# New places in the round for the small pieces of a batch, and shifted values copied by DMA

## The chip, the cores and the metric

The kernel runs on one core of a Trainium2 chip. The metric is the time of one execution on the device, in microseconds; three runs of the kernel before gave 1841.18, 1840.72 and 1837.23 us, median 1840.72. One further execution was profiled.

## What is computed

One transformer layer in float32 on 8 batches of 1024 tokens with 128 features: a relative-position attention with 8 heads of 16 features, then a mixture of 8 experts of which each token uses two.

```python
xh = xn.reshape(b, s, H, Dh)
q = xh @ Wq + bq
k = xh @ Wk + bk
v = xh @ Wv + bv
p = pe @ Wp
content = jnp.einsum('bqhd,bkhd->bhqk', q + u_bias, k)
pos_score = jnp.einsum('bqhd,khd->bhqk', q + v_bias, p)
pos_score = _rel_shift(pos_score)
attn = jax.nn.softmax((content + pos_score) / jnp.sqrt(jnp.float32(e)), axis=-1)
ctx = jnp.einsum('bhqk,bkhd->bqhd', attn, v).reshape(b, s, e)
x = x + ctx @ Wo + bo
```

After it, for each token, a small router (a projection to 64 features, a normalization, a GELU, 8 logits, the best two of them) and, for each expert, `(x1 * gelu(x2)) @ W2`, weighted and added to x. The relative shift moves each row of the position scores by one more column than the row above; along the diagonal it needs, for each key, the value of the token behind it ("shifted values", the values of tokens 1 to 1024 in the places 0 to 1023).

## The kernel before, in words

The program has a prologue, an attention loop of 8 rounds (one for each batch), a tail, and an expert phase that the change doesn't touch. The loop is one body, written out and repeated with a branch. A round is written as 8 heads `h` of 9 units `u`; a place `(h, u)` in the tables is a unit of the round. In every unit all engines have their own list of work in the same order:

- TensorE (block `pe`): `second_pass` computes two halves of 512 scores into `pB` for the softmax of head h (L612 to L626), and `first_pass` two pieces of 512 scores of head h + 2 into one of three banks `pA` (L586 to L604), in turns. In the units 1, 4, 6 and 8 (`PAIRS_AT`, L217) 16 context matmuls (L637) follow, which weigh the values with the probabilities of two key blocks. The units 0, 2, 3, 5 and 7 have no context matmuls. In unit 8 the first pass is 8 small matmuls (L604).
- ScalarE (`act`): two exponentials of 512 columns (L906, L908) out of `pB` into one of four probability buffers, or into `upper_diag` in unit 0.
- VectorE (`v`): reads each `pA` bank with a mask and keeps maxima (L974, L980 in unit 8); TensorE waits before `first_pass` for the bank it writes (`s1_read`).
- GpSimd (`po`): masks the diagonal blocks (L487 to L499), and issues DMAs: `store` (L427, the operands of the next batch to DRAM) and `scatter` (L452, rows of tokens to their experts).
- SyncE (`sp`): loads the operands of a head three heads ahead (`stack`), the row of maxima (`maximum_row`), the odd and even rows exchanged (`swap`, L249), x in and out.

Between these each round has its small pieces, at places set by tables (L178 to L216). The larger ones on TensorE: "turn" (transposes of the context), "project" 0 and 1 in the table `W_ORDER` and `M_ORDER` (the output projection, L667), "shifted" (values of the tokens moved by one, L573), eight pieces of `project()` for the next batch (two transposes L547, then q, p and k in halves of 512 columns, L550), all in head 2 in the units 0 to 7; "rows", "hidden", "fold", "logits", "ranks" of the router (L675 to L702), `upper_form` (L557), "super" (L561) and "values" (L567). The small ones are "row" (L578, the maxima of a head) and "context" (L583). Pieces write one of two banks, `pM` or `pE`. Each has a reader on ScalarE or VectorE, and TensorE waits in its queue until the bank was read (`m_done`, `w_done`, `e_done`) before the next piece for that bank. ScalarE reads pieces (`evacuate`, L811 to L818; `copied`, L840 and L848) ahead of the exponentials of the unit after the piece.

On VectorE, `normalized` (L1007 to L1015) works on the context of the batch before in head 0; its last step, at (0, 7), multiplies `vsh` by `den` (L1015). `router_apply` (L1043) scales the tokens for the router, two tiles each at (2, 5) to (2, 8), `low` (L958) makes the low parts of the operands, `stats` and `normalize` belong to the layer norm of the next batches. On GpSimd `residual` (L431, at (0, 6)) adds the bias to the residual, `positions` (L410 to L417) rotates, `rstd` (L385 to L397) takes inverse roots in head 7.

The engines meet only at semaphores. TensorE and the others execute strictly in the order written, so a place in a table is a place in every queue.

## Time and profile before

| | us |
|---|---|
| median of three runs | 1840.72 |
| profiled execution | 1844.59 |
| its span, first to last instruction | 1843.0 |
| TensorE busy in the span | 1640.6 |
| VectorE busy | 1439.7 |
| ScalarE busy | 1087.3 |
| GpSimd busy | 1145.3 |
| mean granted TensorE clock | 0.929 of 2.4 GHz |

The attention loop begins near 103 us (the second exponential of its first unit) and its last exponential ends at 1357.8 us; the rest of the span is the prologue, the tail of the attention and the expert phase. Times in the trace are counted from the start of the span. A unit is delimited here by the start of its second exponential (L908) and of the next unit's. The matmuls of TensorE are recorded with an overlap, so its busy share near 100% says that it had work, not that its array was full; idle time of an engine and what ended it stand behind an instruction in the timeline.

### The profile page before, as it was taken

How to read it: one execution, taken by the hardware profiler on the slowest of the kernel's cores; microseconds unless marked ns; L12 is line 12 of the kernel's file. 1: busy time of each engine (PE TensorE's matmuls, PEld its weight loads, DVE VectorE, ACT ScalarE, POOL GpSimd, SP SyncE). 2: the span in 40 equal slices, each digit the busy share in tenths (PEclk: the TensorE clock that was granted, in tenths of full speed). 3: DMA queues.
4: the chain of work that ended last, by engine and by line, in shares of the span. 5: the costliest groups of instructions: out<-in, count | busy, mean ns of one | idle time of the engine just before them, and what ended most of it. 6: DMA issues, size and time to landing. Idle time of an engine off the chain costs nothing. (4 is left out here: it accounts for less than half of the span.)

```text
span 1843.0 us, 50545 instructions
## 1 busy us (share of the span) xinstructions
PE 1640.6 (89%) x12522; PEld 1246.7 (68%) x12523; DVE 1439.7 (78%) x5415; ACT 1087.3 (59%) x2162; POOL 1145.3 (62%) x2136
## 2 busy tenths in 40 slices
PE   2689999999999999999999999999962699999997
PEld 1466666666676666667666666766641599999997
DVE  3578978988888887898889789888964477777775
ACT  2046666655665665666566566656630466666665
POOL 4156666767657676765766667576673266665665
PEclk8579999998998999999899999999975799999999
DMA  4425523633643363264256236426444233333333
GB/s 162 153 79 144 141 77 111 157 104 91 155 99 103 109 158 97 83 154 115 83 136 150 75 89 160 107 79 171 114 131 131 42 49 52 52 48 51 52 48 45
DMA packets 138828, 191.53 MB, mean 104 GB/s; under 512 B 27424, under 2 KB 102064, under 8 KB 138576
## 3 DMA queue, kind: packets, MB, share of 16 engines
q1 hardware_dynamic: 91088, 126.67, 25.1%
q0 software_dynamic: 47488, 61.99, 17.2%
q8 instruction: 99, 1.62, 0.4%
q14 instruction: 153, 1.25, 0.2%
HBM read 108.24 MB, written 75.06 MB: 99 GB/s over the span
## 5 line engine op out<-in xcount | busy, mean ns | idle before, releaser
L974 DVE CUSTOM_DVE_ANT_0 junk<-pA,lmask 128x512 bf16<-128x512 f32 x1056 | 689.7, 682 | 184.9 <-PE pA L598 93.3
L1443 POOL DMA_INDIRECT out<-yb,dst x144 | 234.2, 1627 | 162.4 <-ACT yb L1517 86.8
L598 PE MATMUL pA<-K,QL 96*128 96x512 f32 (+3 forms) x792 | 290.2, 368 | 16.2 <-DMA K<-split_operands 14.9
L906 ACT ACTIVATE prob<-pB 128x512 f32<-128x512 f32 x384 | 229.1, 597 | 111.2 <-PE pB L619 86.3
L621 PE MATMUL pB<-QL,K 97*128 97x512 f32 (+3 forms) x768 | 286.6, 373 | 0.0
L619 PE MATMUL pB<-QU,K 97*128 97x512 f32 (+3 forms) x640 | 270.5, 423 | 5.4 <-ACT b_all L906 2.9
L600 PE MATMUL pA<-K,QU 96*128 96x512 f32 (+3 forms) x660 | 245.5, 373 | 26.5 <-DVE acc L974 18.8
L637 PE MATMUL pC<-prob,vext 128*32 128x256 f32 x3088 | 231.9, 405 | 1.5 <-POOL prob L499 1.5
L908 ACT ACTIVATE prob<-pB 128x512 f32<-128x512 f32 x384 | 229.1, 596 | 3.5 <-PE pB L621 2.8
L499 POOL TENSOR_TENSOR prob<-prob,upper_diag 128x128 f32<-128x128 f32 x384 | 185.8, 484 | 32.3
L452 POOL DMA_INDIRECT routed_rows<-rows_r,idx x156 | 158.0, 1013 | 51.0 <-issue 26.7
L619 PEld LDWEIGHTS pB<-QU,K 97*128 97x128 f32 x640 | 123.4, 193 | 94.8 <-issue 35.6
L598 PEld LDWEIGHTS pA<-K,QL 96*128 96x128 f32 x792 | 157.1, 198 | 38.6 <-DMA K<-split_operands 15.2
L600 PEld LDWEIGHTS pA<-K,QU 96*128 96x128 f32 x660 | 136.0, 206 | 50.9 <-DVE acc L974 32.7
L1555 DVE SCALAR_TENSOR_TENSOR g<-pLin,b_all,gl 128x256 f32<-128x256 f32 x292 | 126.0, 478 | 53.5 <-PE pLin L1466 51.2
L621 PEld LDWEIGHTS pB<-QL,K 97*128 97x128 f32 x768 | 153.2, 199 | 15.4 <-issue 3.9
L492 POOL MEMSET prob<- 1x1 f32 x384 | 34.7, 90 | 189.8 <-ACT prob L908 188.0
L637 PEld LDWEIGHTS pC<-prob,vext 128*32 128x32 f32 x3088 | 90.2, 114 | 87.5 <-issue 36.7
L1510 ACT ACTIVATE gl<-pGate,b_all 128x256 f32<-128x256 f32 x292 | 122.2, 470 | 45.3 <-PE pGate L1466 45.1
L1472 PE MATMUL pY<-w_all,g 128*128 x1152 | 140.4, 275 | 0.0
L487 POOL TENSOR_SCALAR_AFFINE_SELECT upper_diag<-upper_diag 128x1024 f32<-128x1024 f32 x64 | 70.0, 1094 | 111.2 <-ACT upper_diag L908 110.2
L1472 PEld LDWEIGHTS pY<-w_all,g 128*128 128x128 f32 x1152 | 134.2, 192 | 0.0
(304 smaller groups left out, 3741.2 us busy)
## 6 DMA issues: line engine op xcount, KB each, us to landing
QL<-split_operands SPq DMA_DIRECT2D x67, 256.0 KB, 3.5
QU<-split_operands SPq DMA_DIRECT2D x67, 256.0 KB, 3.9
K<-split_operands SPq DMA_DIRECT2D x67, 256.0 KB, 4.1
xg<-routed_rows SPq DMA_DIRECT2D x76, 132.0 KB, 2.2
QL<-split_operands SPq DMA_DIRECT2D x67, 128.0 KB, 3.5
QU<-split_operands SPq DMA_DIRECT2D x67, 128.0 KB, 3.8
K<-split_operands SPq DMA_DIRECT2D x67, 128.0 KB, 3.9
split_operands<-c_h POOLq DMA_DIRECT2D x16, 512.0 KB, 6.2
```

Of the source, the lines that this page charges most:

```text
L452: po.indirect_dma_start(dram["xs"], bass.IndirectOffsetOnAxis(idx[:, t, j:j + 1], 0), rows[:, t, :], None).then_inc(scattered, 16)
L499: po.tensor_tensor(p, p, upper_diag[h % 2][:, P * kb:P * kb + P], ALU.add).then_inc(p_mask, 1)
L598: mm = pe.matmul(dst[:, 0:low], QL[0:KROWS, s, q], K[0:KROWS, s, k0:k0 + low], start=True, stop=True)
L600: mm = pe.matmul(dst[:, low:HALF], QU[0:KROWS, s, q], K[0:KROWS, s, k0 + low:k0 + HALF], start=True, stop=True)
L619: mm = pe.matmul(pB[:, q0:q0 + up], K[0:r, s, k], QU[0:r, s, q0:q0 + up], start=True, stop=True)
L621: mm = pe.matmul(pB[:, q0 + up:q0 + HALF], K[0:r, s, k], QL[0:r, s, q0 + up:q0 + HALF], start=True, stop=True)
L637: mm = pe.matmul(pC[VW * strip:VW * strip + VW, :], vext[:, kb, h % H, :], prob[kb % RING][:, quarter * strip:quarter * strip + quarter], ...
L906: act.activation(p[:, 0:HALF], pB[:, 0:HALF], ACT.Exp, scale=SCALE).then_inc(p_exp, 1)
L908: act.activation(p[:, HALF:S], pB[:, HALF:S], ACT.Exp, scale=SCALE).then_inc(p_exp, 1)
L974: v.tensor_tensor_reduce(junk[:, n % S1_BUFS, :], pA[n % S1_BUFS][:, :], lmask[:, at:at + HALF], 1.0, -3.0e38, ALU.add, ALU.max, acc[:, s, ...
L1443: po.indirect_dma_start(dram["out"], bass.IndirectOffsetOnAxis(dst[k][:, a:a + 1], 0), yb[k][:, a, :], None, compute_op=ALU.add).then_inc( ...
L1472: mm = pe.matmul(pY[k % 2][:, a, :], g[k % 2][:, c, P * a:P * a + P], keep["w2"][:, bass.ds(ex * F + c * E, E)], start=(c == 0), stop=(c = ...
```

## The change

- Pieces are listed in two tables `M_AT` and `W_AT` by name, each with its place or places; the places where ScalarE and VectorE read them are in tables of their own (`ACT_OUT`, `DVE_OUT`). All places are units without context matmuls, except those of "row" 1, 3, 4, 6 and 7. ScalarE reads a piece behind the exponentials of a unit instead of ahead of them.
- q, p and k of the next batch (`project` 2 to 7), `upper_form`, "values" and "super" are issued in two halves, in two units. `project` is spread over heads 0 to 2; its two transposes move to head 7 of the round before, at (7, 3) and (7, 5), and with them the layer norm of the batch (`LN_AT`, heads 5 to 7; `RSTD_AT`, heads 3 and 4).
- The eight matmuls for shifted values (L573) and the two ScalarE copies out of them go. "values" is copied once, contiguous, to `held`, which now has all 8 heads; `values_placed` copies from there to `vext`, four heads at (6, 4) and four at (0, 6); and two DMAs of SyncE in head 2 copy `held` to `vsh`, one partition up.
- `residual` moves from (0, 6) to (1, 1), the four tiles of `router_apply` are done at once at (3, 1) and (3, 4), and `positions`, `store`, `scatter`, `low`, `high` and the router's steps move by some units.
- SyncE loads `xt` at head 0 (before: head 2), and at head 2 does `swap`, the copies to `vsh` and the write of x ahead of `maximum_row(3)`.
- Prologue and tail follow: the prologue also normalizes batch 1 and does its two transposes.

```diff
-        held = sb("held", [P, NB, H // 2, D])
+        held = sb("held", [P, NB, H, D])
...
-        placed = sem("last_heads_values")
+        placed, moved = sem("head_values_placed"), sem("values_shifted")
...
-        M_ORDER = {(h, u): name for h in range(H) for u, name in ((1, "row"), (3, "context"))}
-        M_ORDER.update({(1, 5): "project 1", (1, 7): "shifted 1", (6, 6): "values 0"})
-        W_ORDER = {(1, 0): "turn 0", (1, 2): "turn 1", (1, 4): "project 0", (1, 6): "shifted 0", (6, 5): "super", (6, 7): "values 1"}
-        W_ORDER.update({(3, 0): "rows 0", (3, 2): "rows 1", (3, 7): "hidden", (5, 0): "fold", (5, 5): "logits", (7, 0): "ranks"})
-        SPREAD = {"super": ((6, 0), (6, 2), (6, 4), (6, 5)), "hidden": ((3, 5), (3, 7))}
-        PARTS = {**{place: (name, 0, 1) for order in (M_ORDER, W_ORDER) for place, name in order.items() if name not in SPREAD},
-                 **{place: (name, i, len(places)) for name, places in SPREAD.items() for i, place in enumerate(places)}}
-        HIGH_AT = ((2, 5), (2, 6), (3, 0), (3, 1), (4, 1), (4, 2))
-        LOW_AT = ((2, 6), (2, 7), (3, 1), (3, 2), (4, 2), (4, 3), (4, 4), (4, 6))
-        UPPER_AT = ((4, 3), (4, 5))
-        POSITIONS_AT = ((2, 7), (2, 8), (3, 1), (3, 3), (3, 5), (3, 7), (5, 2), (5, 4))
+        M_AT = {"row 1": ((0, 1),), "context 7": ((0, 3),), "turn 0": ((1, 0),), "turn 1": ((1, 2),), "out 0": ((1, 5),), "out 1": ((1, 7),),
+                "context 0": ((2, 0),), "row 3": ((2, 1),), "context 1": ((2, 3),), "row 4": ((3, 1),), "rows 0": ((3, 3),), "rows 1": ((3, 5),),
+                "context 2": ((3, 7),), "hidden": ((4, 0), (4, 2)), "row 5": ((4, 5),), "context 3": ((4, 7),), "row 6": ((5, 1),), "fold": ((5, 3),),
+                "context 4": ((5, 5),), "logits": ((6, 0),), "row 7": ((6, 1),), "context 5": ((6, 3),), "ranks": ((6, 7),), "row 8": ((7, 2),),
+                "context 6": ((7, 3),)}
+        W_AT = {"row 2": ((1, 5),), "values 0": ((4, 5), (4, 7)), "values 1": ((5, 5), (5, 7)), "super": ((6, 0), (6, 2))}
+        ACT_OUT = {"turn 0": (1, 1), "turn 1": (1, 4), "rows 0": (3, 4), "rows 1": (3, 6), "values 0": (4, 8), "fold": (5, 4), "values 1": (5, 8)}
+        DVE_OUT = {"row 1": (0, 2), "context 7": (0, 4), "out 0": (1, 6), "row 2": (1, 6), "out 1": (2, 0), "context 0": (2, 1), "row 3": (2, 2),
+                   "context 1": (2, 4), "row 4": (3, 2), "context 2": (3, 8), "hidden": (4, 4), "row 5": (4, 6), "context 3": (4, 8), "row 6": (5, 2),
+                   "context 4": (5, 6), "logits": (6, 1), "row 7": (6, 2), "context 5": (6, 4), "super": (6, 4), "ranks": (7, 1), "row 8": (7, 3),
+                   "context 6": (7, 4)}
+        PROJECT_AT = {2: ((0, 0), (0, 2)), 3: ((0, 5), (0, 7)), 4: ((1, 2), (1, 3)), 5: ((1, 7), (2, 0)), 6: ((2, 2), (2, 3)), 7: ((2, 5), (2, 7)),
+                      0: ((7, 3),), 1: ((7, 5),)}
+        PROJECT_OUT = {2: (0, 4), 3: (0, 8), 4: (1, 4), 5: (2, 1), 6: (2, 4), 7: (2, 8), 0: (7, 4), 1: (7, 6)}
+        UPPER_AT, UPPER_OUT = (((3, 2), (3, 3)), ((3, 7), (4, 0))), ((3, 4), (4, 1))
+        SPLITS = (("c", 0), ("c", 1), ("k", 0), ("k", 1), ("gu", 0), ("gl", 0), ("gl", 1), ("gu", 1))
+        HIGH_AT = {(1, 6): 0, (1, 8): 1, (2, 6): 2, (3, 1): 3, (3, 6): 5, (3, 8): 6}
+        LOW_AT = {(2, 3): 0, (2, 5): 1, (2, 7): 2, (3, 2): 3, (3, 6): 4, (4, 1): 5, (4, 3): 6, (4, 4): 7}
+        POSITIONS_AT = ((2, 2), (2, 4), (2, 5), (2, 6), (2, 8), (3, 1), (5, 4), (5, 6))
...
-        STATS_AT, AGGREGATE_AT, APPLY_AT, ROOT_AT = ((2, 0), (2, 1)), (2, 2), ((2, 5), (2, 6), (2, 7), (2, 8)), (2, 3)
-        HIDDEN_AT, HIDDEN_ROOT_AT, NORM_HIDDEN_AT = ((4, 0), (4, 1)), (4, 2), ((4, 5), (4, 7))
-        CUBE_AT, TANH_AT, GELU_AT, TOP_AT, EXP_AT = (5, 2), (5, 3), (5, 4), ((5, 6), (5, 7), (5, 8)), (6, 3)
-        SCATTER_AT = ((7, 3), (7, 4), (7, 7), (7, 8), (0, 1), (0, 3), (0, 5), (0, 8), (1, 0), (1, 1), (1, 2), (1, 4), (1, 5), (1, 6), (1, 7), (1, 8))
+        LN_AT = ((5, 3), (5, 4), (5, 6), (6, 2), (6, 3), (6, 5), (6, 7), (7, 0))
+        RSTD_AT = ((3, 3), (3, 5), (3, 7), (3, 8), (4, 0), (4, 1), (4, 2))
+        RESIDUAL_AT, LAST_HEADS_AT, FIRST_HEADS_AT = (1, 1), (0, 6), (6, 4)
+
+        STATS_AT, AGGREGATE_AT, APPLY_AT, ROOT_AT = ((2, 1), (2, 4)), (2, 6), ((3, 1), (3, 4)), (2, 7)
+        HIDDEN_AT, HIDDEN_ROOT_AT, NORM_HIDDEN_AT = ((4, 6), (4, 7)), (4, 8), ((5, 1), (5, 2))
+        CUBE_AT, TANH_AT, GELU_AT, TOP_AT, EXP_AT = (5, 5), (5, 6), (5, 7), ((6, 1), (6, 4), (6, 6)), (6, 8)
+        SCATTER_AT = ((7, 4), (7, 6), (0, 3), (0, 4), (0, 5), (0, 6), (0, 8), (1, 0), (1, 2), (1, 3), (1, 4), (1, 5), (1, 6), (1, 7), (1, 8), (2, 1))
...
-        STORE_AT = {(3, 0): ("c", 0), (3, 2): ("c", 1), (3, 4): ("k", 0), (4, 4): ("gl", 0), (4, 7): ("gu", 0)}
-        READY = {"c": 2, "k": 4, "gl": 6, "gu": 8}
+        STORE_AT = {(3, 2): ("c", 0), (3, 4): ("c", 1), (3, 6): ("k", 0), (4, 5): ("gl", 0), (4, 6): ("gu", 0)}
+        READY = {"c": 2, "k": 4, "gl": 7, "gu": 8}
...
                     if h == 0:
-                        written = known(sp, b * 16 + 16)
-                        sp.wait_ge(set_dve, DVE_SET)
-                        sp.wait_ge(d_x2, written)
-                        sp.dma_start(xres[:, :, :], dram["x"][bass.ds((b + B - 1) % B, 1)].rearrange("o (t p) e -> p (o t) e", p=P)).then_inc(d_res, 16)
-                    if h == 2:
-                        normed = known(sp, (b + 2) * LN_N)
+                        written, normed = known(sp, b * 16 + 16), known(sp, (b + 2) * LN_N)
                         sp.wait_ge(set_dve, DVE_SET)
                         sp.wait_ge(ln, normed)
                         sp.dma_start(xt[:, :, :], dram["x"][bass.ds((b + 2) % B, 1)].rearrange("o (t p) e -> p (o t) e", p=P)).then_inc(d_x, 16)
+                        sp.wait_ge(d_x2, written)
+                        sp.dma_start(xres[:, :, :], dram["x"][bass.ds((b + B - 1) % B, 1)].rearrange("o (t p) e -> p (o t) e", p=P)).then_inc(d_res, 16)
...
+                    if h == 2:
+                        swap(b + 1)
+                        sp.wait_ge(m_ready, m_at(b, "turn 1") + 1)
+                        sp.wait_ge(placed, b * 2 + 2)
+                        sp.dma_start(vsh[0:P - 1, :, :, :], held[1:P, :, :, :]).then_inc(moved, 16)
+                        sp.dma_start(vsh[P - 1:P, 0:NB - 1, :, :], held[0:1, 1:NB, :, :]).then_inc(moved, 16)
+                        sp.wait_ge(m_done, m_at(b, "out 1") + 1)
+                        sp.dma_start(dram["x2s"][bass.ds(b, 1)].rearrange("o (t p) e -> p (o t) e", p=P), xres[:, :, :]).then_inc(d_x2, 16)
+                    if h + 1 == 2:
+                        sp.wait_ge(w_done, w_at(b, "row 2") + 1)
+                    else:
+                        sp.wait_ge(m_done, m_at(b, f"row {h + 1}") + 1)
...
+            def project(nb, j, part=0, parts=1):
...
+                    lo, hi = HALF * part // parts, HALF * (part + 1) // parts
+                    at = HALF * (j % 2)
+                    mm = pe.matmul(dst[:, lo:hi], w[:, :], src[:, at + lo:at + hi], start=True, stop=True)
+                if part == parts - 1:
+                    mm.then_inc(e_ready, 1)
...
-            def values_shifted(half):
-                for t in range(4):
-                    c = P * (4 * half + t) + 1
-                    mm = pe.matmul((pE, pM)[half][:, P * t:P * t + P], xnT[:, c:c + P], w_v[:, :], start=True, stop=True)
-                return mm
-
...
                 if name.startswith("values"):
-                    src = src[:, :].rearrange("p (t h d) -> p t h d", t=4, d=D)
-                    act.activation(vext[:, four, 0:H // 2, 0:D], src[:, :, 0:H // 2, :], ACT.Copy)
-                    dst, src = held[:, four, :, :], src[:, :, H // 2:H, :]
+                    dst, src = held[:, four, :, :].rearrange("p t h d -> p (t h d)"), src[:, :]
                 elif name.startswith("rows"):
                     dst, src = hT[:, HALF * half:HALF * half + HALF], src[:, :]
-                elif name.startswith("turn"):
+                else:
                     dst, src = ctxT[:, HALF * half:HALF * half + HALF], src[:, :]
-                else:
-                    dst, src = vsh[:, four, :, :].rearrange("p t h d -> p t (h d)"), src[:, :].rearrange("p (t e) -> p t e", e=E)
                 act.activation(dst, src, ACT.Copy).then_inc(done, 1)
 
+            def values_placed(heads):
+                act.activation(vext[:, :, heads, 0:D], held[:, :, heads, :], ACT.Copy).then_inc(placed, 1)
```

## Rows read from the trace of the kernel before

**Rows 1.** Page, busy us (share of the span) and instructions of each engine.

```profile
PE 1640.6 (89%) x12522; PEld 1246.7 (68%) x12523; DVE 1439.7 (78%) x5415; ACT 1087.3 (59%) x2162; POOL 1145.3 (62%) x2136
```

**Rows 2.** Windows: us, busy us (instructions) of five engines, clock, DMA, GB/s; two rounds.

```profile
1207.09:1357.80 150.71, 145.33 (x1135) 102.01 (x1138) 131.47 (x537) 99.27 (x192) 102.28 (x232) 0.98 0.46 116
417.08:575.63 158.55, 151.25 (x1158) 105.89 (x1158) 133.82 (x549) 100.25 (x193) 105.94 (x238) 0.95 0.44 114
```

**Rows 3.** Windows, as rows 2: the eight heads of the round from 417.08.

```profile
417.08:435.86 18.78, 17.57 (x127) 11.41 (x126) 16.54 (x46) 11.04 (x21) 14.51 (x27) 0.88 0.20 55
435.86:457.89 22.03, 21.49 (x168) 16.46 (x169) 17.80 (x75) 12.46 (x25) 16.84 (x35) 0.92 0.30 84
457.89:479.81 21.92, 21.39 (x148) 13.55 (x147) 18.92 (x79) 17.18 (x33) 11.68 (x29) 1.00 0.41 121
479.81:502.29 22.48, 20.72 (x152) 15.44 (x153) 18.17 (x74) 12.65 (x25) 16.64 (x35) 0.85 0.81 193
502.29:520.47 18.18, 17.65 (x132) 11.57 (x132) 18.11 (x80) 12.48 (x25) 12.59 (x30) 1.00 0.52 114
520.47:537.86 17.39, 17.24 (x140) 12.06 (x140) 15.57 (x81) 12.18 (x23) 10.52 (x26) 1.00 0.56 144
537.86:556.69 18.83, 18.58 (x160) 14.33 (x159) 14.06 (x59) 11.60 (x26) 7.41 (x24) 1.00 0.26 66
556.69:575.63 18.94, 16.61 (x137) 11.07 (x137) 14.64 (x63) 10.68 (x20) 15.76 (x35) 0.98 0.45 122
```

**Rows 4.** Windows, as rows 2: units (1, 8), (7, 5), (7, 6) and (7, 8).

```profile
455.16:457.89 2.73, 2.73 (x31) 2.07 (x30) 2.20 (x19) 1.30 (x4) 2.49 (x5) 1.00 0.77 229
565.55:566.83 1.28, 1.22 (x7) 0.89 (x6) 1.28 (x5) 1.10 (x4) 1.10 (x3) 1.00 1.04 312
566.83:569.04 2.21, 2.21 (x23) 1.21 (x21) 1.31 (x5) 1.08 (x4) 2.12 (x5) 1.00 0.28 92
570.41:575.63 5.22, 3.03 (x31) 2.31 (x31) 2.52 (x19) 1.29 (x3) 4.03 (x10) 0.94 0.58 153
```

**Rows 5.** Windows, as rows 2: units (1, 1), (1, 5), (1, 6), (1, 7) and (2, 2).

```profile
437.99:442.17 4.18, 4.13 (x24) 2.52 (x25) 2.83 (x9) 1.58 (x4) 3.61 (x5) 0.59 0.28 81
448.23:450.07 1.84, 1.84 (x15) 1.69 (x14) 1.84 (x6) 1.08 (x4) 0.89 (x4) 1.00 0.11 37
450.07:453.32 3.25, 3.25 (x33) 2.45 (x32) 2.63 (x8) 1.56 (x5) 2.68 (x5) 1.00 0.06 21
453.32:455.16 1.84, 1.84 (x18) 1.79 (x16) 1.41 (x8) 1.57 (x4) 0.87 (x4) 1.00 0.11 37
462.21:464.89 2.68, 2.25 (x9) 1.28 (x8) 2.68 (x16) 2.23 (x6) 0.80 (x3) 1.00 0.19 73
```

**Rows 6.** Timeline: start us, us, engine, line, out<-in [idle before <-releaser]; end of head 0.

```profile
431.69 2.37 POOL L431 TENSOR_TENSOR xres<-xres,bo_rows 128x1024 f32<-128x1024 f32 x1
...
432.18 2.96 DVE L1015 TENSOR_TENSOR vsh<-vsh,den 128x1024 f32<-128x1024 f32 x1
...
436.04 0.50 PE L600 MATMUL pA<-K,QU 96*128 96x512 f32 x1 [0.98 <-DVE acc L980]
```

**Rows 7.** Timeline, as rows 6: the same L1015 after the last round.

```profile
1367.45 1.22 DVE L1015 TENSOR_TENSOR vsh<-vsh,den 128x1024 f32<-128x1024 f32 x1
```

**Rows 8.** Timeline, as rows 6: a projection; tiles for the router; start of head 3.

```profile
474.36 0.59 DVE L1043 TENSOR_SCALAR rows_r<-xres,mv_r,rs_r 128x128 f32<-128x128 f32 x2
...
475.06 1.02 PE L550 MATMUL pE<-xnT,w_k 128*128 128x512 f32 x2
...
476.67 1.73 POOL L410 TENSOR_TENSOR g_lo<-rp,cos_lo 128x512 f32<-128x512 f32 x1
...
477.19 1.57 DVE L1043 TENSOR_SCALAR rows_r<-xres,mv_r,rs_r 128x128 f32<-128x128 f32 x2
...
483.06 0.80 PE L600 MATMUL pA<-K,QU 96*128 96x512 f32 x1 [1.76 <-DVE acc L974]
```

**Rows 9.** DMA issues: out<-in, queue, op xcount, KB each, median us to landing.

```profile
rq<-rp SPq DMA_DIRECT2D x18, 256.0 KB, 3.0
```

389 lines of the change are left out of this document (197 added, 192 removed).

## Prediction

> **What bounds the kernel now.** I read the page first: TensorE is busy for 89% of the span and VectorE for 78% [rows 1]. Both are means over the attention loop and the expert phase, so I cut the loop into rounds, a round into heads, and a few heads into units. A round takes between 150.7 us (the last, which has no branch back behind it) and 158.6 us with the same instructions [rows 2]. In the slow one TensorE is busy for 151 us and VectorE for 134, so TensorE sets the end, but it also loses time that the fast round doesn't lose.
>
> By heads [rows 3]: heads 0 to 3 take 18.8, 22.0, 21.9 and 22.5 us, head 5 17.4. TensorE is busy nearly throughout in heads 1 and 2; VectorE is in head 4 (18.11 of 18.18).
>
> By units [rows 4]: one without context matmuls takes 1.28 us when it is bare, and ScalarE is busy for 1.10 of it; one with them takes 2.21 with the same 1.08 of ScalarE and 1.31 of VectorE. So in the first kind the three engines are level, in the second TensorE is alone. A large piece of some 1.0 us of matmuls tells them apart: in (1, 6), with context matmuls, "shifted 0" brings 3.25 - 2.21 = 1.04 us; in (1, 5) "project 1" brings 1.84 - 1.28 = 0.56, in (1, 7) "shifted 1" about as much [rows 5]. A unit of the first kind hides some 0.45 us of a piece.
>
> **The lost time.** (1, 1) takes 4.18 us at a mean granted clock of 0.59 [rows 5]: most of it at 1.2 GHz. Before it TensorE stood for 0.98 us, waiting for VectorE, which was late because L1015 took 2.96 us beside GpSimd's L431 of 2.37 us [rows 6]. After the loop, away from L431, the same L1015 takes 1.22 us [rows 7]. L431 ends at 434.06; 1.22 us later is 435.28, and L1015 ends at 435.14: it stood until L431 was over. The Trainium skill states such a rule (SBUF — State Buffer, "Who interferes with whom"): a VectorE instruction with two inputs in SBUF contends with a GpSimd one that reads SBUF, and whoever starts first blocks the other for its whole length; this trace agrees, with 2.96 against 1.22 us.
> The second place is the start of head 3: a pair of L1043 takes 0.59 us alone and 1.57 beside L410, the next stands ahead of the first passes of head 3, and TensorE waits for 1.76 us [rows 8]; head 3 has a mean clock of 0.85 [rows 3]. The third is the branch at the end of (7, 8), 5.22 us against 2.73 in (1, 8) [rows 4]; it stays. What do the first two cost? The round without either takes 150.7 + 2.5 for a branch = 153.2, the one with both 158.6 [rows 2], so 2.7 us each.
>
> **The change, head by head**, against the round from 417.08 [rows 3]. A bare head is head 7 without its last unit, 570.41 - 556.69 = 13.7, with a last unit of 2.73 [rows 4]: 16.45 us.
> - Price of a half piece. A whole projection takes 1.02 us [rows 8], a half so 0.51, of which a unit without context matmuls hides up to 0.45. Bounds 0.06 and 0.51; I take 0.2, nearer to the lower one as the measured units are nearer to it. The reading by ScalarE now stands behind the exponentials, mostly in units with context matmuls, where ScalarE has 1.1 us free [rows 4]. Where it now stands ahead of the next exponential in (2, 2), the unit takes 2.68 us of which ScalarE is busy for 2.23 [rows 5]; that goes. Two readings of q (2.68 - 1.28 = 1.40, 0.7 us each) or the two of "fold" exceed the free 1.1 by some 0.3: I charge 0.3 in heads 0, 1 and 5.
> - Head 0: four halves. The first runs at 1.2 GHz after the branch: 1.0, the others 0.6; readings 0.3. L1015 no longer stands beside L431: -0.9, the wait of TensorE. 18.8 + 1.0 = 19.8.
> - Head 1: the shifted pieces go, -1.0 and -0.5; "out 0" leaves a unit with context matmuls, 1.04 to 0.56, -0.5; that makes -2.0. Three halves +0.6, readings +0.3. The rest of the wait before it -0.4; (1, 1) at 2.4 GHz, 4.18 to 2.5, -1.7. 22.0 - 3.2 = 18.8. The cover is GpSimd: it is busy 16.84 us in this head, now has L431's 2.37 and one scatter less (1 us), 18.2 of 18.8. It may be up to 1.9 us behind, as the context matmuls use a block two units after its exponential; if the cover goes, each further us is paid in full.
> - Head 2: a bare head, five halves (1.0) and "context 0" (0.1): 17.6 against 21.9. VectorE loses its eight L1043 and gets one `low` and `final`: 18.9 less some 2.8 is 16.1, no bound.
> - Head 3: bare, two "rows" of 0.6 us of which one shares a unit with a half, three halves, together 1.2: 17.7. VectorE now has all eight L1043, 0.3 to 0.8 each, on top of a head's own work; I take its 18.4. "rows 1" at (3, 5) waits for the four of (3, 4), and behind that wait stand all scores. A wait of 1 to 2 us is possible here, none to the other side.
> - Head 4: bare, "hidden" in two units 0.9, the half beside it 0.5, two halves of values 0.4: 18.2, as before. Head 5: bare, "fold" 0.2, two halves 0.4, readings 0.3: 17.3. Head 6: "logits" 0.6, with half of "super" in the same unit 0.8, the other half 0.4: 18.2. Head 7: 18.9 + 0.3 for the transposes: 19.2.
> - `rstd` moves beside `positions` in heads 2 to 4, where GpSimd has 16.6 us at most of 22 [rows 3], and leaves head 7: no cost taken, up to 1 us if the masks come late. The two copies to `vsh` are issued in head 2; the nearest transfer lands in 3.0 us [rows 9], and the data are used in head 0 of the next round, 100 us later. On the SyncE queue `swap`, these copies and the write of x now stand ahead of `maximum_row(3)`, used a head (18 us) later: nothing. Prologue and tail: nothing, within 3 us, as the prologue waits for stored operands anyway.
>
> **The sum.** 19.8 + 18.8 + 17.6 + 18.4 + 18.2 + 17.3 + 18.2 + 19.2 = 147.5 us a round, against a mean of (1357.8 - 103 + 2.5)/8 = 157.2. Two allowances: a wait with its slow clock comes back in every second round (2.7/2 = 1.3), and the 14 handoffs of a bank that now stand close together cost 0.1 each (1.4; lower bound 0, upper 0.7 each, the length of one ScalarE reading). 150.2 us. The gain is 7.0 a round, 56 for eight. The profiled execution of 1844.6 becomes 1788.6; it stands 3.9 above the median, so the forecast is 1785.
>
> **Rivals.**
> (a) *All of it arrives*: no allowance is needed, 9.7 a round: 1763.
> (b) *VectorE keeps the pace, and the waits stay.* It has the same 132 us of work a round [rows 2], and four L1043 at once are a longer block than two: by the same rule of the Trainium skill (same page and section; 0.98 us more for a pair beside L410 in this trace [rows 8]) each group can stand for one GpSimd instruction. Then the stop at head 3 stays or moves to (3, 5), and the even spread gives nothing. Left are the shifted pieces (1.5), and the freed L1015 with its slow unit (2.7), less 1.0 for the first half at 1.2 GHz: 3.2 a round, 1815. For it speaks head 4, which is VectorE's already; against it, that head 2 loses more on VectorE than head 3 gains.
> (c) *Slower: the handoffs.* Fourteen steps on `pE` (8 projections, 2 upper forms, "row 2", 2 values, "super") have a wait of TensorE for a reader that now comes a unit later, and all scores queue behind. If 14 of them cost the upper 0.7 us each, that is 9.8 a round against a gain of 7.0 + 1.4 without their allowance: +1.4 a round, 1852. It decides from 0.6 each on. Against it: TensorE reaches a piece one unit's scores (1 us) after the exponentials, and the reading ends sooner in all but three places.
> (d) *The copy doesn't come in time* or disturbs the loads of the operands: 1 MB more through a queue whose engines are busy for less than half of the time [rows 2]; it would cost the wait of one `stack`, and leaves the forecast's case.
>
> **How the numbers follow.** Forecast with (a) 0.66 (1760 to 1803), (b) 0.23 (1803 to 1832), (c) 0.07, no difference 0.04. The range takes the first, the larger part of (b), and the bounds of the half piece (0.06 to 0.51 for 22 halves, -3 to +7 a round, of which the rest of a unit hides a part): 1760 to 1826. Faster by over 0.2% 0.89, within 0.2% (about what a measurement of this kernel can tell from no change) 0.04, slower 0.07.
>
> **What the profile after would show.** L1015 at 1.2 to 1.7 us and (1, 1) at a clock of 1.0; no L573; head 2 near 17.6 and head 1 near 18.8 us; (3, 1) without a wait of TensorE; units with half pieces near 1.5. I am wrong if GpSimd ends the idle time of L637 in head 1, if TensorE waits at (3, 5) and runs at 1.2 GHz behind it, or if a half piece costs its full 0.5 us.

## The result, and the profile after

The changed kernel takes 2032.3 us (median of four runs, 2024.3 to 2042.5) against 1841.0 for the kernel before: a ratio of 1.104, with a 95% interval of 1.098 to 1.111. The forecast was 1785 us, faster; the changed kernel is 191 us slower than the kernel before and 247 us above the forecast. Times here and below are medians over each kernel's runs; one run of four of e2_spread_stores, 1905.5 us, fell in a slower state of the chip and is left out. In the profiled execution of the changed kernel the span is 2037.4 us. The page has the work of before [rows 1] and 41 us more of it on TensorE, in a span that is 194 us longer (busy us, share, instructions):

```profile
PE 1681.4 (83%) x12530; PEld 1308.4 (64%) x12531; DVE 1444.2 (71%) x5423; ACT 1091.8 (54%) x2139; POOL 1147.1 (56%) x2138
```

So hardly anything was added to do: the 194 us are time in which TensorE stands, or does the same work at a lower clock (mean granted clock 0.869, before 0.929). The windows (columns as in rows 2) of the last round and of the one from 465.96 us, and below them the eight heads of the latter, answer to [rows 2, 3]:

```profile
1376.74:1553.94 177.20, 153.05 (x1129) 110.76 (x1129) 131.92 (x531) 99.27 (x187) 105.32 (x235) 0.86 0.36 97
465.96:648.08 182.12, 155.89 (x1158) 113.32 (x1158) 134.35 (x550) 100.55 (x191) 106.26 (x238) 0.87 0.38 102
...
465.96:484.55 18.59, 18.48 (x136) 12.99 (x136) 16.21 (x57) 13.44 (x25) 13.55 (x29) 0.91 0.13 37
484.55:503.27 18.72, 18.72 (x156) 14.34 (x155) 15.83 (x70) 12.89 (x25) 16.82 (x32) 1.00 0.32 90
503.27:536.37 33.10, 18.30 (x140) 13.93 (x140) 17.87 (x75) 12.65 (x24) 18.82 (x34) 0.81 0.39 117
536.37:555.84 19.47, 19.20 (x142) 13.80 (x142) 17.56 (x64) 13.63 (x27) 15.12 (x35) 0.88 0.50 120
555.84:581.66 25.82, 19.56 (x154) 14.91 (x154) 17.01 (x74) 11.48 (x23) 14.51 (x33) 0.87 0.62 162
581.66:600.90 19.24, 18.19 (x140) 12.67 (x140) 16.87 (x66) 12.83 (x25) 10.44 (x26) 0.90 0.30 80
600.90:625.42 24.52, 24.34 (x161) 17.82 (x161) 17.47 (x88) 11.52 (x23) 7.46 (x24) 0.72 0.20 50
625.42:648.08 22.66, 19.10 (x136) 12.85 (x136) 15.53 (x65) 12.11 (x23) 9.54 (x26) 0.90 0.47 129
```

Several things are to be seen. Head 1 is as forecast (18.7 us for 18.8), head 0 is 1.2 us below (18.6 for 19.8). The window of head 2 lasts 33.1 us and TensorE is busy for only 18.3 of them. Head 4 has a hole of 6 us, and heads 5 to 7 run at a mean clock of 0.72 to 0.90, where before they ran at 0.98 and more.

The view of the waits of TensorE (for what: us in total, times, the longest) names both kinds of loss, the transfer of the row of maxima and, as "issue", something that no instruction released:

```profile
PE pB L637 <- DMA QU<-mrow: 161.9, 17, 14.0
PE pB L637 <- issue: 18.0, 7, 3.3
```

In the kernel before, the first of these is one wait of 3.3 us in the whole execution. Where it comes from is seen in the timeline of the SyncE queue (start, duration of the issue, tile) around the long wait:

```profile
508.47 0.71 SPq L319 DMA_DIRECT2D vsh<-held  x1
509.22 0.65 SPq L320 DMA_DIRECT2D vsh<-held  x1
510.13 8.48 SPq L322 DMA_DIRECT2D out<-xres  x1
518.73 9.85 SPq L274 DMA_DIRECT2D QL<-mrow  x1
528.64 0.67 SPq L274 DMA_DIRECT2D QU<-mrow  x1
...
533.84 1.11 PE L637 MATMUL pB<-QU,K 97*128 97x128 f32 x4 [13.98 <-DMA QU<-mrow]
```

The two issues behind the copies of the shifted values take 8.48 and 9.85 us, where they take 0.44 and 0.70 in e1_spread, the first experiment below. The row of maxima is therefore sent at 528.64, and TensorE, which stands ahead of head 3 from 519.86 on, goes on at 533.84. In the other rounds it is the small second copy whose issue is long (8.3 to 9.4 us), and then one of the row or both; in each round TensorE goes on some 25.3 us behind the issue of the first copy. What holds up the queue is the copy itself, as the experiments show. The page's DMA issues (KB each, median us from issue to landing) of the changed kernel show the write of x, which is issued behind the copy, at 14.9 us; in the kernel before it is 4.6:

```profile
out<-xres SPq DMA_DIRECT2D x9, 512.0 KB, 14.9
```

In the trace's packet records the copy of 127 rows shows as packets of 4096 bytes that come one at a time: from 512 to 530 us there are 113 of them, 0.161 us each, each beginning as the one ahead of it ends (within 0.01 us). So one of the 16 DMA engines moves them, and 127 such packets take some 20 us (127 x 0.161 = 20.4). The records that were kept don't name the engine. A write of 128 rows, the one of x, lands in 4.6 us in the kernel before, so it can't go at that pace. The Trainium skill has the rule (DMA: Bandwidth & Descriptors, "Why a DMA increments its semaphore by 16 and not by 1"): such a transfer is dealt to as many engines, up to 16, as divide its slowest dimension, and 127 partitions go to a single one. The trace agrees, with its packets of 4096 bytes one behind the other.

### The profile page after: what moved, and what is told of

It reads as the page before. It is cut to its first block and busy times, and to the rows that moved or that the text cites. A ratio compares the mean times of both kernels' runs of the same rounds, so it can differ in the third digit from the quotient of the medians.

```text
span 2037.4 us, 50549 instructions
## 1 busy us (share of the span) xinstructions
PE 1681.4 (83%) x12530; PEld 1308.4 (64%) x12531; DVE 1444.2 (71%) x5423; ACT 1091.8 (54%) x2139; POOL 1147.1 (56%) x2138
## 5 line engine op out<-in xcount | busy, mean ns | idle before, releaser
L610 PE MATMUL pA<-K,QL 96*128 96x512 f32 (+3 forms) x792 | 297.8, 378 | 8.0 <-DVE acc L1000 4.8
L633 PE MATMUL pB<-QL,K 97*128 97x512 f32 (+3 forms) x768 | 303.2, 395 | 0.0
L612 PE MATMUL pA<-K,QU 96*128 96x512 f32 (+3 forms) x660 | 260.8, 396 | 0.5 <-DVE acc L1000 0.3
L637 PE MATMUL pB<-QU,K 97*128 97x128 f32 x512 | 97.2, 323 | 179.9 <-DMA QU<-mrow 161.9
L649 PE MATMUL pC<-prob,vext 128*32 128x256 f32 x3088 | 243.3, 423 | 0.0
L637 PEld LDWEIGHTS pB<-QU,K 97*128 97x128 f32 x512 | 91.7, 240 | 208.2 <-issue 208.2
L631 PEld LDWEIGHTS pB<-QU,K 97*128 97x128 f32 x640 | 124.6, 195 | 98.3 <-issue 63.3
L913 ACT ACTIVATE upper_diag<-pB 128x512 f32<-128x512 f32 x64 | 38.2, 597 | 273.4 <-PE pB L637 273.4
L610 PEld LDWEIGHTS pA<-K,QL 96*128 96x128 f32 x792 | 166.8, 211 | 24.9 <-DVE acc L1000 11.8
L633 PEld LDWEIGHTS pB<-QL,K 97*128 97x128 f32 x768 | 162.4, 211 | 12.0
L612 PEld LDWEIGHTS pA<-K,QU 96*128 96x128 f32 x660 | 148.1, 225 | 19.5 <-DVE acc L1000 6.2
```

The source lines that it names most:

```text
L610: mm = pe.matmul(dst[:, 0:low], QL[0:KROWS, s, q], K[0:KROWS, s, k0:k0 + low], start=True, stop=True)
L612: mm = pe.matmul(dst[:, low:HALF], QU[0:KROWS, s, q], K[0:KROWS, s, k0 + low:k0 + HALF], start=True, stop=True)
L631: mm = pe.matmul(pB[:, q0:q0 + up], K[0:r, s, k], QU[0:r, s, q0:q0 + up], start=True, stop=True)
L633: mm = pe.matmul(pB[:, q0 + up:q0 + HALF], K[0:r, s, k], QL[0:r, s, q0 + up:q0 + HALF], start=True, stop=True)
L637: mm = pe.matmul(pB[:, k], K[0:r, s, k], QU[0:r, s, k], start=True, stop=True)
L649: mm = pe.matmul(pC[VW * strip:VW * strip + VW, :], vext[:, kb, h % H, :], prob[kb % RING][:, quarter * strip:quarter * strip + quarter], ...
```

## The experiments

Each ratio is against the kernel before in the same comparison, with its 95% interval. The heads below are means over six middle rounds, from the start of the second exponential of a head's first unit to that of the next head's; so the stop ahead of head 3 is in the column of head 2, and the branch in that of head 7. The row "forecast" is the prediction's sum by heads, without its allowances of 2.7 us a round. The heads are of the profiled execution, the ratios of all runs.

```
us by head         0     1     2     3     4     5     6     7    round   ratio
kernel before    18.7  21.6  21.9  21.6  18.2  17.4  18.8  19.4   157.7
forecast         19.8  18.8  17.6  18.4  18.2  17.3  18.2  19.2   147.5
changed          19.2  18.7  33.1  19.7  26.0  20.1  21.5  23.5   181.7   1.104
e1_spread        18.6  18.7  18.0  22.2  26.0  20.0  19.6  22.9   166.0   1.039
e17_spread_pad   17.0  18.7  18.0  21.2  25.9  19.5  19.1  19.9   159.3   1.018
e15_spread_whole 17.2  18.3  19.1  18.2  26.4  19.9  19.8  19.0   157.9   1.011
e14_repaired     17.2  18.3  18.4  19.1  19.3  21.4  18.1  21.7   153.5   0.987
e8_shift_residual 16.5 19.4  21.9  21.1  18.2  17.4  18.8  16.9   150.2   0.971
e18_apply_earlier 16.6 19.4  21.9  20.0  18.2  17.4  18.8  16.8   149.1   0.967
```

### e1_spread: the copy in two pieces of 112 and 15 rows

```diff
-                        sp.dma_start(vsh[0:P - 1, :, :, :], held[1:P, :, :, :]).then_inc(moved, 16)
+                        for lo, hi in ((0, 112), (112, P - 1)):
+                            sp.dma_start(vsh[lo:hi, :, :, :], held[lo + 1:hi + 1, :, :, :]).then_inc(moved, 16)
```

> Edit: the copy of held to vsh (127 partitions) is issued as 112 and 15 partitions. Theory A (the 127-partition copy is served by one transfer engine: the write of x and the row of maxima behind it are held up, 8.5 and 9.9 us to issue against 0.9 and 0.7 before, and TensorE waits 14.0 us at the start of head 3): the copy takes about 127 x 0.167 / 16, under 2 us, the 14.0 us go in each round, and with them the slow clock behind them: 14 to 17 us a round, 2032 to 1900 - 1920. Rival B (the order of the SyncE queue, with the row of maxima behind swap, out 1 and the write of x, is what makes it late): nothing but the copy's own part changes, 2020 to 2032. Rival C (the 1 MB more of traffic): the same bytes move, no change.

Measured: 1914.5 us, ratio 1.039 (1.035 to 1.043). The same 127 rows of 4 KB go through the same queue at the same place, and 118 us of the 191 are gone. So neither the order of the queue nor the bytes made the difference. The issues of the DMA page and the waits of e1_spread:

```profile
out<-xres SPq DMA_DIRECT2D x9, 512.0 KB, 3.3
vsh<-held SPq DMA_DIRECT2D x8, 448.0 KB, 3.7
```

```profile
PE pB L638 <- DMA QU<-mrow: 50.2, 9, 6.2
```

The copy lands in 3.7 us, the write behind it in 3.3. Of the 17 long waits for the row of maxima 9 are left. Those are of another place, the end of head 4.

### e3_two_engines: the copy in pieces of 122 and 5 rows

> Edit: as e1_spread, but 122 and 5 partitions. Theory A with its rule that a copy is spread over the largest number up to 16 that divides its rows (122 = 2 x 61: two engines): 61 x 0.167 = 10.2 us instead of 21.2, so the wait at head 3 falls from 14.0 to about 3 us: 1925 to 1945. If any split would do (16 engines as in e1_spread): equal to e1_spread. If it is the order of the queue: 2020 to 2032.

Measured: 1938.2 us in one run, as expected. The time follows the number of engines that the split allows by the rule above: one for the largest piece 2032, two 1938, sixteen 1914. The waits of e3_two_engines:

```profile
PE pB L638 <- DMA QU<-mrow: 88.5, 17, 6.3
```

161.9 us in the changed kernel, 88.5 here, 50.2 with the copy spread: 112, 38 and 0 us of it belong to the copy, 14, 5 and 0 in each of eight rounds (about 3 were expected for the second).

### e12_shift_one_engine: the one-engine copy in the kernel before

The kernel before with the shifted values by DMA as in the change, and nothing else of it.

```diff
-        M_ORDER.update({(1, 5): "project 1", (1, 7): "shifted 1", (6, 6): "values 0"})
+        M_ORDER.update({(1, 5): "project 1", (6, 6): "values 0"})
...
                     if h == 2:
                         swap(b + 1)
+                        sp.wait_ge(w_ready, b * W_N + W_OF["turn 1"] + 1)
+                        sp.wait_ge(placed, b + 1)
+                        sp.dma_start(vsh[0:P - 1, :, :, :], held[1:P, :, :, :]).then_inc(moved, 16)
+                        sp.dma_start(vsh[P - 1:P, 0:NB - 1, :, :], held[0:1, 1:NB, :, :]).then_inc(moved, 16)
```

> The kernel before with the shifted values by DMA, the copy as one of 127 rows (e7_shift_alone has it as 112 and 15): the price of the one-engine copy without anything of the new placement. Theory C (one engine moves the 127 rows in 21 us, and the row of maxima that is issued behind it comes late): TensorE waits 12 to 15 us at the start of head 3, head 3 goes from 21.4 to 34 to 36 us, 1801 becomes 1900 to 1920. Rival (the wait came from where the new placement has the row of maxima and the residual's store): under 3 us in head 3, about 1815.

Measured: 1914.3 us, ratio 1.036 (1.031 to 1.041); with the copy as 112 and 15 rows (e7_shift_alone, next) it is 1801.0. The one-engine copy costs 113 us in the old placement too, so it owes nothing to the new one. Here it isn't the row of maxima that is held up first but the load of the operands issued ahead of it (two issues, 16.27 us together); waits and the SyncE queue of e12_shift_one_engine:

```profile
PE pB L625 <- DMA QU<-mrow: 104.4, 9, 17.2
```

```profile
663.57 1.26 SPq L320 DMA_DIRECT2D out<-xres  x1
665.17 16.27 SPq L257 DMA_DIRECT2D QL<-split_operands  x2
...
684.12 0.75 SPq L264 DMA_DIRECT2D QL<-mrow  x1
```

### e7_shift_alone: the shifted values by DMA, the copy spread, in the kernel before

> The kernel before with one part of the change: the shifted values are copied by DMA (as 112, 15 and 1 partitions, behind swap in head 2) instead of by 8 matmuls and 2 ScalarE copies; values are copied to held for all heads. Forecast's term: 1.04 + 0.47 us a round less in (1, 6) and (1, 7), 12 us: 1830. Rival: VectorE or the clock takes it back: 1838 to 1845.

Measured: 1801.0 us, ratio 0.975 (0.971 to 0.978). Faster by 47 us, where the terms of the prediction for it add up to some 12 (1.5 a round for the shifted pieces). Head 1 gives 1.8 us a round (21.6 to 19.8), as expected. The rest is at the branch: head 7 takes 17.0 us for 19.4 and head 0 17.2 for 18.7. The first work of TensorE behind the branch, in the timeline of the kernel before and of e7_shift_alone:

```profile
574.00 0.32 PE L625 MATMUL pB<-QU,K 97*128 97x128 f32 x1 [2.19 <-issue]
```

```profile
557.06 0.33 PE L626 MATMUL pB<-QU,K 97*128 97x128 f32 x1
```

and the windows of its heads 7 and 0, at a clock of 1.00 in both, where [rows 3] has 0.98 and 0.88:

```profile
541.77:558.85 17.08, 16.61 (x137) 10.79 (x136) 14.47 (x63) 10.57 (x20) 14.72 (x34) 1.00 0.46 114
558.85:576.13 17.28, 15.62 (x126) 10.55 (x126) 16.72 (x46) 10.94 (x22) 15.47 (x29) 1.00 0.38 97
```

So the stop of 1.8 to 3.2 us at each of the seven branches back, which the prediction took as given, is gone with the shifted pieces. Their instructions are what left TensorE's loop. The changed kernel took them out as well and kept its stop; its halves had put as many back. That made a question of its own.

### e4_residual_alone and e8_shift_residual: L431 away from L1015

```diff
-                        if (h, u) == (0, 6):
+                        if (h, u) == (1, 1):
                             residual(b)
```

> The kernel before with one edit: residual moves from (0, 6) to (1, 1). Theory P (of the prediction: L1015 is held up by L431): L1015 falls from 2.96 to 1.2 - 1.7 us, the wait of 0.98 us and the slow clock in (1, 1) go in all rounds that have it: 2.7 a round in 6 of 8, 16 to 22 us less than before, 1819 to 1825. Rival: VectorE is late there anyway and another of its instructions beside GpSimd's takes the time: no change, 1841.

> e7_shift_alone and e4_residual_alone together. If the two gains add (9 us measured for the residual alone, 12 expected for the shift): 1818 to 1825. If GpSimd, which now does L431 in the shorter head 1, sets the pace there: the shift's part is lost, 1833.

Measured: 1833.8 us for the first, ratio 0.995 (0.992 to 0.997); 1793.0 for the second, ratio 0.971 (0.968 to 0.974), 8 us under e7_shift_alone. L1015 takes 1.22 us in every round, also in e4_residual_alone:

```profile
429.08 1.22 DVE L1015 TENSOR_TENSOR vsh<-vsh,den 128x1024 f32<-128x1024 f32 x1
...
436.17 2.36 POOL L431 TENSOR_TENSOR xres<-xres,bo_rows 128x1024 f32<-128x1024 f32 x1
```

The mechanism is as predicted (0.98 us of waiting and the slow clock behind it, [rows 6]), its size is not: 8 to 10 us of the execution, 1 to 1.2 a round, where the prediction had 2.7. In the six middle rounds of the profiled execution head 0 goes from 18.7 to 18.3 and head 1 from 21.6 to 20.6. (That execution, 1824.3 us, is the fastest of the seven, whose median is 1833.8; head 3 is 1.1 us shorter in it too.) Head 1 gives back a part: unit (1, 1) falls from 3.7 to 2.4 us in the mean, but (1, 4) rises from 3.2 to 4.1, in e4_residual_alone as in e8_shift_residual. Its second group of context matmuls (L637, at 440.62) has 0.22 us of waiting for GpSimd's mask (L499) ahead of it, where the kernel before has none: L431 at (1, 1) has put GpSimd behind. That is the cover that the prediction named, and it is used up here. In the changed kernel, with "out 0" no longer in that unit, (1, 4) takes 2.3 us without a wait.

### e10_pad_loop, e11_pad_ahead, e13_before_pad: what decides the stop at the branch

Needless small matmuls (128 by 8 elements, into a bank that the next work overwrites): in e10_pad_loop one ahead of each turned context, in the loop; in e11_pad_ahead eight, once, ahead of the loop; both on e8_shift_residual. In e13_before_pad it is the kernel before, with nothing but this:

```diff
+            for _ in range(56):
+                pe.matmul(pC[:, 0:8], ident[:, :], ident[:, 0:8], start=True, stop=True)
             pe.wait_ge(e_done, E_N)
```

> The kernel of e8_shift_residual with one needless small matmul ahead of each turned context, 8 a round (16 matmuls and 16 loads in the record, as many as the shifted pieces had). Theory L (length of TensorE's loop): the stop at the branch, none in e8, is back with 1.8 to 3.3 us, with 1.2 GHz behind it: heads 7 and 0 go from 16.9 and 16.5 to 19.3 and 18 us, and with up to 1 us for the matmuls themselves the time is 1820 to 1832. Theory W (the stop comes from another engine or from transfers, and left with the shifted pieces because VectorE and ScalarE had less to do): no stop, 1793 to 1801.

> The kernel of e8_shift_residual with the same 8 needless matmuls once, ahead of the loop. They move the loop in TensorE's program and leave its length. If it is the place of the branch or of its target that decides, the stop at the branch is back: 1815 to 1825. If it is the length of the loop, nothing: 1793 within 3 us.

> The kernel before with 56 needless small matmuls ahead of the loop, where TensorE waits anyway (224 recorded instructions, which move the branch from the 2998th to the 3222nd). So far there was no stop with the branch at the 2964th and 2981st, and one with it at the 2996th, 2998th and 3013th. Theory P (what counts is where the branch falls in a pattern that repeats every 256): 3222 is to 256 what 2966 is, so no stop, heads 7 and 0 become 17 and 17 us, and 1841 becomes 1812 to 1820, with nothing else changed. Theory T (a fixed place from which on a branch back is dear): the stop stays with 1.8 to 3.3 us, 1841 to 1848.

Measured: 1827.9 us for e10_pad_loop (ratio 0.991, 0.988 to 0.993), 1819.1 for e11_pad_ahead (0.989, 0.983 to 0.994) and **1809.8 for e13_before_pad** (0.982, 0.978 to 0.986). The waits of TensorE of the first two:

```profile
PE pB L627 <- issue: 22.0, 7, 3.4
```

```profile
PE pB L628 <- issue: 19.6, 7, 3.4
```

In e13_before_pad there is no such row. Counted in the records of TensorE and its sequencer (matmuls, weight loads, register steps, waits), the first branch back is the 2964th in e7, e8, e12, e16 and e18, the 2981st in e9, e14 and e15, the 3221st in e17 and the 3222nd in e13_before_pad: no stop in any. It is the 2996th in e10_pad_loop and e11_pad_ahead, the 2998th in the kernel before and e4, the 3013th in the changed kernel and in e1, e2, e3, e5 and e6: a stop in all, of 1.8 to 3.4 us. e11_pad_ahead has the loop of e8_shift_residual unchanged (2719 records) and stops; e13_before_pad has the loop of the kernel before (2753) and doesn't. So it isn't the length of the loop, nor what the loop does, but where the code lies in TensorE's program. The padding moves the loop's first record along with the branch; but in the kernel before and in e7_shift_alone that first record is the same one, the 245th (2998 - 2753 and 2964 - 2719), and only the first stops. So it is not the start alone; the place of the branch goes with the stops in all runs. A fixed limit is excluded by 3221 and 3222, which are free behind 2996 to 3013, which are not; they are 256 on from 2965 and 2966, and were chosen for that. A period of 256 agrees with all runs and isn't shown by them: it was tried in one further block alone, and other periods would do as well.

The Trainium skill says (Runtime: NRT & Kernel Launch, "Instruction fetch mechanics") that an engine's instructions arrive in blocks of 256, and that a taken branch to a target outside the blocks at hand waits for a fetch. A period of 256 would fit the blocks. But a wait at every such branch isn't what the runs show: the target is some 2700 records back in all of them, and at four of the seven positions TensorE doesn't stand. There the measurement decides.

Theory L (the loop's length) falls with e11_pad_ahead, and e13_before_pad shows that a kernel can gain 1.8% by moving its code, with some needless work added and nothing taken away.

### e9_whole, e15_spread_whole, e17_spread_pad: what the halves cost

```diff
-        PROJECT_AT = {2: ((0, 0), (0, 2)), 3: ((0, 5), (0, 7)), 4: ((1, 2), (1, 3)), 5: ((1, 7), (2, 0)), 6: ((2, 2), (2, 3)), 7: ((2, 5), (2, 7)),
+        PROJECT_AT = {2: ((0, 2),), 3: ((0, 7),), 4: ((1, 3),), 5: ((2, 0),), 6: ((2, 3),), 7: ((2, 7),),
...
-        UPPER_AT, UPPER_OUT = (((3, 2), (3, 3)), ((3, 7), (4, 0))), ((3, 4), (4, 1))
+        UPPER_AT, UPPER_OUT = (((3, 3),), ((4, 0),)), ((3, 4), (4, 1))
```

The first has this on e6_waits (below), the second on e1_spread; the third is e1_spread with its halves and 52 of the small matmuls ahead of the loop.

> The kernel of e6_waits with the six split projections and the two upper forms whole again, each at the place of its second half. Theory H (a half is cheap, a whole piece dear, as in the prediction's step: 0.2 us a half against 0.57 a whole one in a unit without context matmuls): 0.17 us more for each of 8 pieces, 1.4 a round, 1883 becomes about 1894. Theory L (the halves put 16 matmuls and 16 weight loads back into TensorE's loop, as many as the shifted pieces took out, and the length of that loop decides whether TensorE stands at the branch): the stop of 2.9 to 3.3 us at the end of head 7 and the slow clock behind it go, head 7 loses some 2.5 and head 0 some 1.5 us, less 1.4 for the whole pieces: 2 to 3 us a round, about 1862.

> The changed kernel with two things undone, the one-engine copy (as in e1_spread) and the halves (as in e9_whole): what these two cost together, with nothing else moved. From e1_spread's 1914, less the 31 us between e6_waits and e9_whole: 1878 to 1888, with no stop at the branch. If more than 1895, the halves did gain something where the places of e1_spread stand.

> The kernel of e1_spread, halves and all, with 52 needless small matmuls ahead of the loop: the branch of TensorE falls to the 3221st recorded instruction, 256 behind the 2965th, where there is no stop. What the halves cost apart from the place of the branch is the difference to e15_spread_whole (1863). Theory F (the halves' whole price was the place of the branch): 1858 to 1870. Theory G (a half costs its full 0.5 us too, as the prediction feared): 8 pieces by some 0.4 us a round more, 26 us: 1885 to 1892.

Measured: 1851.8 us for e9_whole (ratio 1.006, 1.003 to 1.009; e6_waits has 1.020), 1862.9 for e15_spread_whole (1.011, 1.007 to 1.015), 1876.3 for e17_spread_pad (1.018, 1.016 to 1.019). From e1_spread's 1.039 the place of the branch alone gives back 2.1%, 38 us. The halves then cost another 0.6%, some 12 us, between what the two theories of e17_spread_pad expected. Where? The window of unit (0, 0) with a half, of e17_spread_pad, and those of (0, 2) and (1, 3) with a whole piece, of e15_spread_whole,

```profile
587.35:588.88 1.53, 1.53 (x8) 1.05 (x7) 1.53 (x5) 1.09 (x2) 0.80 (x1) 1.00 0.61 145
```

```profile
585.58:587.43 1.85, 1.85 (x9) 1.20 (x8) 1.85 (x7) 1.09 (x3) 0.79 (x3) 1.00 0.25 89
604.66:606.41 1.75, 1.75 (x9) 1.18 (x7) 1.48 (x7) 1.11 (x3) 1.59 (x4) 1.00 0.00 0
```

stand against 1.28 of a bare one [rows 4]: 0.25 us for a half (0.34 against the 1.19 that (0, 0) takes without a piece in e15_spread_whole), 0.5 to 0.6 for a whole piece. Over all six projections, from the units of both traces (means of the six middle rounds): the unit that gets a first half is longer by 0.01 to 0.44 us, 0.23 in the mean, and the unit with the second half is shorter by 0.21 to 0.46 than with the whole piece, 0.41 in the mean. That is near the 0.2 and 0.57 of the prediction, and heads 0 to 2 together are 0.9 us a round shorter with halves (53.7 for 54.6). The loss is in head 3, 21.2 against 18.2 us: the first half of the upper form stands at (3, 2), ahead of GpSimd's rotation, and all scores behind it (timeline of e17_spread_pad):

```profile
647.18 1.01 PE L576 MATMUL pE<-g_lo,to_upper 128*128 128x256 f32 x2 [2.32 <-POOL g_lo L434]
```

### e2_spread_stores, e5_positions, e6_waits, e14_repaired: the places of heads 3 to 7

The second kind of wait for the row of maxima, at the end of head 4, has no copy near it. In the changed kernel GpSimd issues the four stores of the gates (512 KB each) between 567.70 and 571.38, and the row of maxima is sent in their midst:

```profile
568.74 0.72 SPq L274 DMA_DIRECT2D QL<-mrow  x1
569.51 2.17 SPq L274 DMA_DIRECT2D QU<-mrow  x1
...
579.12 1.11 PE L637 MATMUL pB<-QU,K 97*128 97x128 f32 x4 [5.75 <-DMA QU<-mrow]
```

In the kernel before the stores stand at (4, 4) and (4, 7), ahead of it and behind it. e2_spread_stores is e1_spread with this:

```diff
-        STORE_AT = {(3, 2): ("c", 0), (3, 4): ("c", 1), (3, 6): ("k", 0), (4, 5): ("gl", 0), (4, 6): ("gu", 0)}
+        STORE_AT = {(3, 2): ("c", 0), (3, 4): ("c", 1), (3, 6): ("k", 0), (4, 7): ("gl", 0), (4, 8): ("gu", 0)}
```

> Edit: e1_spread, and the stores of gl and gu move from (4, 5), (4, 6) to (4, 7), (4, 8). Theory D (the 5.9 us that TensorE waits at the start of head 5 are the row of maxima 5, read at (4, 6) and queued in the transfer engines behind 2 MB of stores issued in the same 3 us): the row lands before the stores are issued, 5.9 us a round less than e1_spread, with a slow clock of 1 to 2 us behind them: 50 to 60 us less than e1_spread. Rival E (the wait is for the head's own last first passes or the stores delay the operands of the head after it): 0, or the wait moves to head 0 of the next round, as the operands stored last are loaded in head 5.

Measured: 1881.6 us, ratio 1.019 (1.016 to 1.022), 33 less than e1_spread, where 50 to 60 were expected. Head 4 goes from 26.0 to 18.9 us, 7 a round or 56 in all; but in the profiled execution (1897.5 us, the slowest of the three) heads 5 and 6 become longer by 1.8 and 4.0. VectorE had caught up while TensorE stood; now TensorE waits for it in head 5 (timeline of e2_spread_stores),

```profile
538.79 0.49 PE L613 MATMUL pA<-K,QU 96*128 96x512 f32 x1 [1.15 <-DVE acc L1001]
...
540.53 0.69 PE L703 MATMUL pM<-ident_f,hr 128*128 128x128 f32 x2 [1.25 <-DVE hr L1098]
```

and runs slowly behind that: the mean clock from 541 to 548 us is 0.61, most of it at 1.2 GHz. Head 6 loses by the clock rather than by waits: (6, 0) to (6, 2) take 10.5 us for 7.8, with a mean clock of 0.58 in the last two, and TensorE waits nowhere in them for over 0.15 us. In this execution most of what was gained in head 4 is given back, by the medians some 40% of it.

e5_positions is e1_spread with the rotation a step earlier:

```diff
-        POSITIONS_AT = ((2, 2), (2, 4), (2, 5), (2, 6), (2, 8), (3, 1), (5, 4), (5, 6))
+        POSITIONS_AT = ((2, 2), (2, 3), (2, 4), (2, 5), (2, 6), (2, 8), (5, 4), (5, 6))
```

> Edit: e1_spread with the six rotation steps of GpSimd at (2, 2), (2, 3), (2, 4), (2, 5), (2, 6), (2, 8) instead of (2, 2), (2, 4), (2, 5), (2, 6), (2, 8), (3, 1). Theory F (TensorE's wait of 2.3 us in (3, 2) is for the last rotation step, which upper_form reads): the wait and the slow clock behind it go: head 3 from 22.2 to about 18.5 us, 3 to 4 us a round, 1914 to 1883 - 1890. Rival G (GpSimd is full in head 2, 16.3 of 18.0 us): its masks come late, the wait moves into the context matmuls of head 2 or 3, and nothing is gained.

Measured: 1908.0 us, ratio 1.032 (1.026 to 1.038). The wait for `g_lo` at (3, 2) is gone and head 3 takes 19.7 us for 22.2; head 6 takes 21.0 for 19.6, and the stops at the branch add up to 18.8 us for 15.6. Of the 20 us that head 3 gives, 6 arrive by the medians and 12 by the ratios; 24 to 31 were expected.

e6_waits is e5_positions with the store of the upper gates at (4, 7), context 4 ahead of "fold", and the cube, the tanh and the logits of the router one or two units later.

> Edit: e5_positions and the other waits of TensorE that the trace of e1_spread shows: the store of gu at (4, 7); fold and context 4 change places, (5, 5) and (5, 3), with the router's steps behind fold one or two units later; logits at (6, 2); out 1 read at (1, 8); context 6 at (7, 5). Theory H (what is left between the changed kernel with a spread copy and the forecast are waits of TensorE for pieces that are not ready, each with slow clock behind it: 5.9 at head 5, 2.3 in (3, 2), 1.0 in (5, 3), 1.5 in (7, 2) and (7, 3), 0.8 in (2, 0)): all go, a round falls from 166 to 150 - 154 us and the time to 1790 - 1815. Rival I (the halves cost what they weigh, TensorE has no more room): waits fall but a round stays above 157, 1840 or more.

Measured: 1882.9 us, ratio 1.020 (1.016 to 1.024). Head 4 takes 21.0, head 5 18.7; head 6 takes 25.8 us, with waits for `mrow`, `lg` and `both` of 0.6, 0.6 and 0.9 us and the slow clock between them. A round takes 162.1 us, so the rival of the expectation holds here: waits fall, and the round stays above 157.

e14_repaired has the spread copy, the whole pieces, the rotation of e5_positions, the stores at (4, 7) and (4, 8), the router's steps behind context 5, and a few small pieces a unit or two earlier or later.

> The changed kernel with all that the runs have named: the copy as 112 and 15 rows, whole projections and upper forms, the stores of the gates at (4,7) and (4,8), the rotation a unit earlier, context 4 ahead of fold, logits behind context 5, ranks and the scatters a unit later. By the heads of the earlier runs, 17.2, 18.3, 18.3, 19.2, 18.9, 18.9, 19.5 and 19.5, a round is 149.9 us, 8.2 less than in e9_whole: 1852 becomes about 1786 if the waits of heads 4 to 7 were due to those places. If the new placement loses there whatever the places are (VectorE behind in each head once TensorE no longer waits), another head becomes longer as head 6 did in e6_waits: 1810 to 1840.

Measured: 1817.7 us, ratio 0.987 (0.983 to 0.992): faster than the kernel before by 23 us, where 56 were forecast. Heads 0 to 4 add up to what the prediction has for them (92.3 us for 92.8, with whole pieces), in part by luck: head 0 is 2.6 under its term, as there is no stop at the branch, and heads 2 to 4 are each 0.7 to 1.1 over theirs. Heads 5 and 7 are far over, 21.4 and 21.7 for 17.3 and 19.2. TensorE's waits of e14_repaired have this row, which in the kernel before is 18.8 us in 24 times:

```profile
PE pA L613 <- DVE acc L999: 32.2, 31, 1.8
```

The rival of that expectation holds: what is taken away as a wait in one head comes back as VectorE's lag in another. The trace says where it begins. TensorE waits for 1.14 us in (5, 3) and for 1.84 us in (7, 1) of each middle round, and runs at a mean clock of 0.5 in the unit behind. Ahead of each, a step of the router on VectorE stands beside GpSimd's mask of 1.09 us (L504): in round 3 the first L1096 takes 1.08 us, 0.30 elsewhere, and L1132 takes 1.00, 0.23 at its shortest, and both end within 0.1 us of the mask. It looks like the contention of L1015 and L1043 once more, at two places that the prediction didn't look at. Whether the waits go with it wasn't tried.

### e16_rotation_later, e18_apply_earlier: the stop at the start of head 3

Both on e8_shift_residual, one constant each.

```diff
-        POSITIONS_AT = ((2, 7), (2, 8), (3, 1), (3, 3), (3, 5), (3, 7), (5, 2), (5, 4))
+        POSITIONS_AT = ((2, 7), (3, 0), (3, 1), (3, 3), (3, 5), (3, 7), (5, 2), (5, 4))
```

> The kernel of e8_shift_residual with GpSimd's second rotation step at (3,0), no longer at (2,8) beside the last pair of L1043. In e8 that pair takes 1.57 and the one before it 1.33 us, and TensorE waits 1.76 us at (3,1) for VectorE. Theory V (that wait is paid as the prediction has it, with its slow clock): the wait falls below 0.8 us, head 3 goes from 21.1 to about 19, and 1793 becomes 1775 to 1783. Rival (the step only meets other work of VectorE there, and the upper form at the end of head 3 comes a unit later): head 3 stays over 20.5, 1790 to 1796.

Measured: 1805.6 us, ratio 0.979 (0.978 to 0.981), 13 us slower than e8_shift_residual. The miss is instructive; timeline of e16_rotation_later:

```profile
620.81 1.10 POOL L494 TENSOR_SCALAR_AFFINE_SELECT upper_diag<-upper_diag 128x1024 f32<-128x1024 f32 x1 [1.31 <-ACT upper_diag L907]
620.92 2.31 DVE L1043 TENSOR_SCALAR rows_r<-xres,mv_r,rs_r 128x128 f32<-128x128 f32 x2
...
621.88 1.27 POOL L417 TENSOR_TENSOR g_lo<-rp,cos_lo 128x512 f32<-128x512 f32 x1
...
624.31 0.50 PE L601 MATMUL pA<-K,QU 96*128 96x512 f32 x1 [2.74 <-DVE acc L973]
```

The pair of L1043, 0.59 us when alone [rows 8], starts just behind the mask L494, stands through it and through the rotation that follows, and ends at 623.23, 0.08 behind L417's end at 623.15. The first of the two instructions ends with the mask (621.99 and 621.91), the second with L417: each stands for one instruction of GpSimd. So it isn't only the rotation that blocks: in e8_shift_residual, where the rotation step was over in time, the same pair takes 1.33 us beside L494 alone. So the pair was taken from both:

```diff
-        STATS_AT, AGGREGATE_AT, APPLY_AT, ROOT_AT = ((2, 0), (2, 1)), (2, 2), ((2, 5), (2, 6), (2, 7), (2, 8)), (2, 3)
+        STATS_AT, AGGREGATE_AT, APPLY_AT, ROOT_AT = ((2, 0), (2, 1)), (2, 2), ((2, 4), (2, 5), (2, 6), (2, 7)), (2, 3)
```

> The kernel of e8_shift_residual with VectorE's four groups of L1043 one unit earlier, (2,4) to (2,7). In e16_rotation_later the last pair stood beside two instructions of GpSimd, L494 (1.10 us) and L417 (1.27), took 2.31 us and ended as L417 did, and the wait of TensorE at (3,1) grew from 1.76 to 2.74. Theory V (VectorE stands behind any GpSimd instruction of that kind, the mask L494 at the start of head 3 too, and the wait at (3,1) is the delay of its last pair): with no pair beside L494 and the first one in VectorE's gap of 1.63 us at (2,4), the wait falls to 0.4 to 1.0 us, head 3 goes from 21.1 to 19 to 20, and 1793 becomes 1777 to 1786. Rival (the pair at (2,7) is then blocked by the second rotation step instead and the delay is only passed on): wait over 1.4 us, 1790 to 1796.

Measured: **1783.8 us**, ratio 0.967 (0.965 to 0.969), the fastest kernel of this study. TensorE's wait is down by 0.75 us (timeline of e18_apply_earlier),

```profile
612.56 0.50 PE L601 MATMUL pA<-K,QU 96*128 96x512 f32 x1 [1.01 <-DVE acc L973]
```

head 3 by 1.1 us, and the time by 9 us, as a stop of 0.75 and its slow clock make in eight rounds.

## Why the prediction was wrong

**The step that failed** is the one on the DMAs. It put the two copies to `vsh` at nothing, because "the nearest transfer lands in 3.0 us" [rows 9] and their data are used 100 us later, and put the SyncE queue behind them at nothing, because the row of maxima is "used a head (18 us) later". The nearest row was not near: it is a transfer of another shape. The copy takes some 20 us, and the issues behind it are held up. Nor were there 18 us to spare. Without the copy the row of maxima would be sent near 511.4 us, in the middle of head 2 (the issues ahead of it take 1.3 us in e1_spread), and TensorE needs it at 519.86: 8.4 us, of which the row needs up to 5.2 itself (528.64 to 533.84). It was held up for 17.2, and TensorE stood for 14.0. That is worth 118 us of the 191 (e1_spread), 113 in the old placement (e12_shift_one_engine). Rival (d) named the right transfer and priced it as "the wait of one `stack`"; it had neither the one engine nor the queue behind it, and its 1 MB is 0.5 MB (127 rows of 4 KB). The slowest dimension of the copy, 127, stood in the diff, and the rule for it in the Trainium skill (the section named above); neither was put beside the other.

**A step that wasn't there**: the stores of the gates. They move from (4, 4) and (4, 7) to (4, 5) and (4, 6), onto the sending of row 5. The working follows `rstd`, the copies and x through the queues, and not these four issues. 7 us in each round's head 4 where it stands (e2_spread_stores), 33 us net.

**The branch.** "The third is the branch ...; it stays" was right for the change and hid the largest single gain within reach: 1.8% by moving the branch (e13_before_pad), 38 us in the changed kernel (e17_spread_pad). The prediction counted the matmuls of the halves as time and not as instructions: 16 matmuls and 16 loads (as recorded) out with the shifted pieces, 16 and 16 in with the halves.

**Price of a half**: right in the mean, 0.23 us for the 0.2 taken (single units 0.01 to 0.44, bounds 0.06 and 0.51). So is what splitting saves: 0.9 us a round in heads 0 to 2, where six pieces by 0.57 less 0.4 make 1.0. The 12 us that the halves lose all the same come from the upper form at (3, 2) ahead of the rotation, a wait that the part on head 3 doesn't have.

**L1015 and L431**: the mechanism right (1.22 us in all rounds of e4_residual_alone, and also of the changed kernel), the size about half or less, 1.0 to 1.2 us a round for 2.7 by the medians, 1.0 to 1.4 by heads 0 and 1 of the traces. A part of it is given back in (1, 4) where the change's other moves are missing.

**Heads 0 to 2**: 18.6, 18.7 and 18.0 us in e1_spread for 19.8, 18.8 and 17.6. The working by unit prices holds to about 1 us a head where TensorE sets the pace. Head 0 is under because the first half, with the slow clock behind the branch, was charged 1.0 us, and units (0, 0) and (0, 1) together take 5.3 us for 5.2 before.

**Head 3**: 18.4 forecast, 22.2 in e1_spread, where the upper form waits for the rotation, 18.2 in e15_spread_whole and 19.1 in e14_repaired. "rows 1" at (3, 5), feared for a wait, has none over 0.3 us in the changed kernel. Of the three signs of being wrong that the prediction named (GpSimd ahead of L637 in head 1, a wait at (3, 5), a half at its full 0.5 us) the changed kernel shows none; it failed at a place for which no sign was named.

**Heads 4 to 7**: 18.2, 17.3, 18.2 and 19.2 forecast, 19.3, 21.4, 18.1 and 21.7 in e14_repaired. Here the sum took bare heads plus matmuls and never asked whether VectorE, with a share of the freed heads' work, keeps the pace. Rival (b) had that, and the contention behind it, at the wrong head: it set the new stop at (3, 5). The allowance, a stop with its slow clock in every second round, was too small; e14_repaired has about four waits of one kind in each round (31 in eight).

**Rival (c)**, the handoffs, foresaw a slower kernel, and slower it was, but for another reason: in the changed kernel the waits of TensorE on `pE` for a reader of the bank stay under 4 us in the whole execution.

**What is open**: from 2032 us down to the forecast of 1785, the copy accounts for 118 us, the place of the branch and the halves for 52 (e15_spread_whole, 1863), the places repaired in e14_repaired for 45, and 33 are left. They lie in heads 5 and 7, which are 4.1 and 2.5 us a round over their terms, and are VectorE's lag there by the waits; no run takes single steps of it away. Nor was it tried where, between the 3013th and the 3221st record, the stop at the branch ends.

## What to carry to other kernels

Before a DMA is put at nothing, look at its slowest dimension (127 rows went one at a time and took some 20 us, 112 and 15 took 3.7) and at the moment at which what is queued behind it is needed, not only at who uses its data. When a wait is taken away, ask which engine had caught up in it: here a good part of what TensorE no longer stood came back in a later head, as VectorE's lag and as the slow clock behind it. And a stop at a loop's branch that no instruction releases can depend on the place of the code alone: before work is rearranged around it, shift the code and measure, since needless instructions ahead of the loop (31 us, e13_before_pad) gave more than the new placement with all its repairs (23 us, e14_repaired).

## What the runs showed of the hardware

- One copy of 127 rows by 4 KB, whose packets go one at a time, holds up the queue of the engine that issued it: in the round shown the issues of the write of x and of the row took 8.48 and 9.85 us instead of 0.44 and 0.70, in another placement two took 16.27 together, and a write of 512 KB behind it landed after 14.9 and 23.3 us (4.6 without the copy).
- Four stores of 512 KB from GpSimd's queue, issued within 4 us, delayed a row of 4 KB on SyncE's queue: TensorE waited for it for some 6 us a round, and not at all with the stores issued behind it.
- TensorE stood for 1.8 to 3.4 us at a branch back with the branch at its 2996th, 2998th or 3013th record, and not at all at the 2964th, 2981st, 3221st or 3222nd. The mean clock of the head behind a stop was 0.88 [rows 3], and 1.00 where there was none.
- A pair of VectorE instructions with one tile as input (L1043, 0.59 us alone) stood for one GpSimd instruction each, a mask with one input and a product with two, and took 2.31 us. The rule with two inputs that the prediction quotes doesn't name this form; the same section of the Trainium skill (SBUF — State Buffer, "Who interferes with whom") does, as it lets `tensor_scalar` too take the pair of ports that GpSimd shares. The measured ends, 621.91 and 621.99, 623.15 and 623.23, agree.
